# A gated Mamba block with routed experts on one core: every batch in halves of 256 steps, narrower TensorE sums and paired GpSimd products

## The reference

```
xi = in_proj_w @ ctx                      # 512 channels
u  = silu(conv4(xi) + conv_b)
x_dbl = x_proj_w @ u                      # dt_lo (16), B (16), C (16)
delta = softplus(dt_proj_w @ dt_lo + b)
state[e,n] = state[e,n]*exp(delta[e]*A[e,n]) + delta[e]*u[e]*B[n]   # each step
y[e] = sum_n state[e,n]*C[n] + D[e]*u[e]
x  = x + tanh(g_xattn) * y * silu(layernorm(x))
```

```
xc = layernorm(x); combine = top2(softmax(xc @ gate_w.T)), shares scaled to sum 1
h  = gelu(wd @ xc + bd) * combine
x  = x + tanh(g_ffn) * (wu @ h + bu + shared expert)
```

## Time and profile before

| | us |
|---|---|
| median of three runs | 680.33 |
| the profiled execution | 678.83 |
| its span (first to last instruction) | 677.1 |
| TensorE matmuls busy (x1772) | 508.2 (75%) |
| VectorE busy (x556) | 509.2 (75%) |
| ScalarE busy (x594) | 347.6 (51%) |
| GpSimd busy (x278) | 496.7 (73%) |
| granted TensorE clock, mean | 0.856 |

### The profile page before, as it was taken

How to read it: one execution, slowest core, us unless ns; L and a number is a source line. 1 busy time by engine, 2 the same in 40 slices (tenths; PEclk the granted TensorE clock), 3 DMA queues, 4 the chain that set the end, 5 groups by cost and what they waited for, 6 DMA issues and landing times.

```text
span 677.1 us, 6131 instructions
## 1 busy us (share of the span) xinstructions
PE 508.2 (75%) x1772; PEld 223.8 (33%) x1772; DVE 509.2 (75%) x556; ACT 347.6 (51%) x594; POOL 496.7 (73%) x278
## 2 busy tenths in 40 slices
PE   5377242323366998797979979787998999998998
PEld 2022010101022333232423423243343344676676
DVE  3553889787889977899999989997688899614311
ACT  2277533343425698634676575533968734265300
POOL 3026999999998969999999999985588969300000
PEclk9586566767588997897999998979898889999799
DMA  8676513031373304234664120263341321200011
GB/s 258 256 255 252 188 58 125 33 122 62 125 248 125 111 25 148 93 117 154 235 213 154 48 78 32 93 233 140 111 135 53 109 74 52 77 1 1 0 55 54
DMA packets 35325, 79.61 MB, mean 118 GB/s; under 512 B 5497, under 2 KB 9145, under 8 KB 35292
## 3 DMA queue, kind: packets, MB, share of 16 engines
q1 hardware_dynamic: 35292, 79.22, 33.8%
HBM read 62.17 MB, written 17.04 MB: 117 GB/s over the span
## 4 chain that ended last, share of the span: by engine, by line
POOL 29%; PE 25%; DVE 19%; issue 18%; ACT 7%; DMA 2%; POOLq 0%; SPq 0%; ACTq 0%; DVEq 0%
POOL ring L834 16%; POOL ring L843 10%; PE wk L1348 10%; DVE decay L1040 5%; PE wk L1334 5%; DVE ring L1040 5%; PE y_ps L1273 4%; PE wk L1289 2%; ACT decay L899 1%; PE wk L1310 1%; DMA b_in<-bc_scratch 1%; POOL dd_out L816 1%; DVE h L1221 1%; DVE ring L1060 1%; ACT h L986 1%
## 5 line engine op out<-in xcount | busy, mean ns | idle before, releaser
L834 POOL TENSOR_TENSOR ring<-dd,b_in 128x1024 f32<-128x1024 f32 x128 | 299.1, 2354 | 13.9 <-DMA dd<-dd_scratch 10.4
L899 ACT ACTIVATE decay<-dd,a_neg 128x511 f32<-128x511 f32 (+2 forms) x320 | 176.5, 590 | 64.2 <-DVE ring L1040 35.1
L843 POOL TENSOR_TENSOR ring<-ring,c_in 128x1024 f32<-128x1024 f32 x64 | 150.4, 2351 | 25.9 <-DVE carry L1052 16.1
L1273 PE MATMUL y_ps<-ring,fold 128*32 128x512 f32 (+1 forms) x640 | 86.0, 677 | 99.4 <-POOL ring L843 97.2
L1040 DVE TENSOR_TENSOR_SCAN ring<-decay,ring 128x1024 f32<-128x1024 f32 x56 | 127.0, 2280 | 20.1 <-ACT decay L899 13.6
L1040 DVE TENSOR_TENSOR_SCAN decay<-decay,ring 128x1024 f32<-128x1024 f32 x56 | 128.0, 2286 | 15.1 <-ACT decay L899 15.1
L1334 PE MATMUL wk<-xc,w_down 128*128 128x512 f32 (+1 forms) x360 | 134.1, 526 | 4.5 <-issue 4.4
L1348 PE MATMUL wk<-h,w_up 128*128 128x512 f32 (+1 forms) x360 | 132.3, 523 | 0.0
L1334 PEld LDWEIGHTS wk<-xc,w_down 128*128 128x128 f32 x360 | 68.0, 194 | 66.8 <-issue 60.8
L1348 PEld LDWEIGHTS wk<-h,w_up 128*128 128x128 f32 x360 | 68.8, 196 | 54.2 <-issue 49.3
L1060 DVE TENSOR_TENSOR ring<-decay,c_in 128x1024 f32<-128x1024 f32 x64 | 78.4, 1225 | 6.7
(11 more groups left out here) (97 smaller groups left out, 441.1 us busy)
## 6 DMA issues: line engine op xcount, KB each, us to landing
dd<-dd_scratch SPq DMA_DIRECT2D x48, 512.0 KB, 3.8
dd<-dd_scratch SPq DMA_DIRECT2D x32, 256.0 KB, 2.9
dd_scratch<-dd_out SPq DMA_DIRECT2D x12, 512.0 KB, 2.9
z<-in_x SPq DMA_DIRECT2D x4, 1024.0 KB, 6.2
x<-in_xT SPq DMA_DIRECT2D x4, 1024.0 KB, 5.8
c_in<-bc_scratch SPq DMA_DIRECT2D x8, 512.0 KB, 4.9
b_in<-bc_scratch SPq DMA_DIRECT2D x8, 512.0 KB, 5.0
x_scratch<-x SPq DMA_DIRECT2D x3, 1024.0 KB, 8.7
```

Source lines behind the costliest of these rows:

```text
L834: nc.gpsimd.tensor_tensor(ring[:, i % RING].rearrange("p (q n) -> p q n", n=n), dd[:, j % DD_RING, None, n:2 * n].broadcast_to([P, TILES[v ...
L843: nc.gpsimd.tensor_tensor(ring[:, i % RING], ring[:, i % RING], c_in[:, g % BC_RING], ALU.mult).then_inc(weighed_pool, 1)
L899: last = nc.scalar.activation(decay[:, i % 2, q * n + first:(q + 1) * n], dd[:, j % DD_RING, first:n], ACT.Exp, scale=a_neg[:, c, r, k:k + 1])
L1273: last = nc.tensor.matmul(y_ps[r * BLOCK:(r + 1) * BLOCK, 0:n], fold[:], ring[:, slots[r] % RING, q * n:(q + 1) * n], start=False, stop=p ...
```

## The change

Three things at once. Every batch is cut into two units of 256 columns, so there are eight units of 16 slots, and all due times are new; `ring` gets 10 slots, `dd_out` 3, `b_in` and `c_in` 2, and GpSimd works four slots ahead. GpSimd handles two slots in one instruction, for the outer products (`outers`) and for the weighing, which is now of `r` = 0 and 1, and copies the carry for its two slots itself. TensorE computes mean, variance and logits as four partial sums in four groups of 32 columns, which ScalarE copies to SBUF and a second matmul adds up, and `D*u` with four 32x32 diagonals. At the start the loads of z and x leave the fixed first group and are placed by the plan behind the first loads of `dd`, as are the biases and the FFN's weights, which stood ahead of all of them. The rest of the diff:

```diff
-UNITS = [(0, 0, 512), (1, 0, 512), (2, 0, 512), (3, 0, 256), (3, 256, 256)]
+UNITS = [(0, 0, 256), (0, 256, 256), (1, 0, 256), (1, 256, 256), (2, 0, 256), (2, 256, 256), (3, 0, 256), (3, 256, 256)]
-RING = 9
+RING = 10
-DD_OUT = 4
-BC_RING = 3
+DD_OUT = 3
+BC_RING = 2
-AHEAD = 3
+AHEAD = 4
-POOL_WEIGHS = (1, 2)
+POOL_WEIGHS = (0, 1)
...
     "load_ffn": [
-        [-12.75, -11.61, -11.52, -11.43, -11.35, -11.26, -11.17, -11.08, -11, -10.91, -10.82],
+        [-1.56, -0.25, 0.07, 0.21, 0.91, 2.61, 3.65, 5.02, 5.39, 5.6, 6.75],
...
     "dt read": [
+        [0.667, 0.75, 0.833, 0.917],
+        [11.4, 11.6, 11.8, 12.5],
+        [21.5, 21.667, 21.833, 23.333],
...
     "silu": [
+        [0.5],
+        [9.333],
+        [20.5],
...
-            def outer(i):
+            def outers(i):
                 v, c, p, r = PLACES[i]
                 j, g, n = block_no(v, c, r), bc_no(v, p), COLS[v]
-                pool.wait_ge(dd_loaded[j % DD_RING], DMA * (j // DD_RING + 1))
+                for k in (j, j + 1):
+                    pool.wait_ge(dd_loaded[k % DD_RING], DMA * (k // DD_RING + 1))
                 pool.wait_ge(b_loaded[g % BC_RING], DMA * (g // BC_RING + 1))
                 if i >= RING:
-                    pool.wait_ge(summed, (i - RING) // NR4 + 1)
...
+                    pool.wait_ge(summed, (i + 1 - RING) // NR4 + 1)
+                nc.gpsimd.tensor_tensor(ring[:, i % RING:i % RING + 2].rearrange("p s (q n) -> p s q n", n=n),
+                                        dd[:, j % DD_RING:j % DD_RING + 2, None, n:2 * n].broadcast_to([P, 2, TILES[v], n]),
...
             def weigh(i):
...
+                if goes_on(v):
+                    j, k = c * NR4 + r, p * TILES[v]
+                    nc.gpsimd.tensor_copy(carry[:, j - 1:j + 1, k:k + TILES[v], None],
+                                          two.rearrange("p s (q n) -> p s q n", n=n)[:, :, :, n - 1:n]).then_inc(carried, 1)
+                    copies[0] += 1
+                    pool.wait_ge(carried, copies[0])
+                nc.gpsimd.tensor_tensor(two, two, c_in[:, None, g % BC_RING].broadcast_to([P, 2, WIDE]),
+                                        ALU.mult).then_inc(weighed_pool, 2)
...
+            def evacuate_sums(name, v):
...
+                nc.scalar.activation(part_sum[:, 0:COLS[v]], wk[:, bank, 0:COLS[v]], ACT.Copy).then_inc(drained[bank], 1)
...
                 else:
+                    if weighs_on_pool(i):
+                        dve.wait_ge(carried, carries(i))
                     for q in range(TILES[v]):
...
-                if goes_on(v):
+                if goes_on(v) and not weighs_on_pool(i):
...
-                    nc.tensor.matmul(y_ps[:, 0:n], d_diag[:, c, :], u[:, w % U_RING, 0:n], start=True, stop=False)
+                    for r in range(NR4):
+                        rows = slice(r * BLOCK, (r + 1) * BLOCK)
+                        nc.tensor.matmul(y_ps[rows, 0:n], d_diag[rows, c, :], u[rows, w % U_RING, 0:n], start=True, stop=False)
...
-                if name == "mean":
+                if name == "mean_p":
                     for j in range(NW):
                         pe.wait_ge(x2_ready, NW * v + j + 1)
-                        last = nc.tensor.matmul(o, mean_w, x2[:, j, cols], start=j == 0, stop=j == NW - 1)
+                        last = nc.tensor.matmul(o[j * BLOCK:(j + 1) * BLOCK, :], mean_w, x2[:, j, cols], start=True, stop=True)
...
+                if name in ("mean", "var"):
+                    wait_drained(pe, name + "_p", v)
+                    last = nc.tensor.matmul(o, group_w, part_sum[:, 0:n], start=True, stop=True)
```

More of the change, by code:

```diff
@@ L103, in weighs, with carries @@
     return sum(weighs_on_pool(j) == pool for j in range(i))
+def carries(i):
+    v, c, p, r = PLACES[i]
+    k = ((p + 1) * TILES[v] - 1) // TILES[v - 1]
+    return sum(goes_on(PLACES[j][0]) and j % NR4 == POOL_WEIGHS[1] for j in range(slot_of(v - 1, c, k, NR4 - 1) + 1))
 def block_no(v, c, r):
@@ L152 @@
+        [84.96, 85.14, 85.66, 86.91],
+        [105.02, 105.16, 106.02, 107.17],
+    ],
+    "mean_p": [
+        [19.22],
+        [33.81],
+        [52.06],
+        [66.64],
+        [82.31],
+        [100.75],
+        [112.9],
+        [131.26],
     ],
     "mean": [
[L154 to L158, removed]
+        [20.59],
+        [34.58],
+        [54.07],
+        [67.36],
+        [83.44],
+        [101.61],
+        [114.4],
+        [132.62],
+    ],
@@ L159 @@
+    "var_p": [
+        [21.36],
+        [35.47],
+        [55.22],
+        [68.93],
+        [84.77],
+        [103.54],
+        [115.48],
+        [133.39],
     ],
     "var": [
[L161 to L165, removed]
+        [22.72],
+        [36.9],
+        [56.67],
+        [70.11],
+        [86.1],
+        [104.83],
+        [118.43],
+        [133.69],
     ],
     "lg_t": [
-        [44.93],
-        [75.18],
-        [104.2],
@@ L342 @@
+        [107.4, 107.6, 107.8, 109.25],
+    ],
+    "mean_p read": [
+        [21.333],
+        [36.5],
+        [54.667],
+        [69.25],
+        [84.667],
+        [103.333],
+        [115.5],
+        [128.053],
     ],
     "square": [
-        [38.5],
-        [74.333],
-        [103.5],
-        [128.03],
-        [128.121],
+        [22.667],
+        [37.2],
+        [57.25],
+        [69.75],
+        [86.333],
+        [104.667],
+        [117.333],
+        [128.105],
+    ],
+    "var_p read": [
+        [23.667],
+        [37.6],
+        [57.75],
+        [71.5],
+        [87.143],
+        [105.667],
+        [117.667],
+        [128.158],
@@ L476, in by_slot @@
     return due
-JOBS = ("in_proj", "x_proj", "dt", "mean", "var", "lg_t", "lg", "comb", "down", "mix", "up")
+JOBS = ("in_proj", "x_proj", "dt", "mean_p", "mean", "var_p", "var", "lg_t", "lg", "comb", "down", "mix", "up")
 PE_ORDER = in_order("y", *JOBS)
 SP_ORDER = in_order("ctx", "z", "x", "xdbl", "dd", "load_dd", "load_b", "load_c", "load_ffn", "x2_store", "x_out", "out")
-POOL_DUE = by_slot("affine_z", "du", "residual")
-ACT_DUE = by_slot("in_proj read", "silu", "x_proj read", "dt read", "square", "var read", "lg_t read", "share_exp",
+POOL_DUE = by_slot("affine_z", "du", "residual", "weigh")
+ACT_DUE = by_slot("in_proj read", "silu", "x_proj read", "dt read", "mean_p read", "square", "var_p read", "var read", "lg_t read", "share_exp",
                   "comb read", "down read", "gelu")
@@ L530, in mamba_moe_kernel @@
         rank = sb("rank", [P, NX])
-        consts = sb("consts", [P, 7])
-        gates = consts[:, 5:7]
-        eps, minus_half, minus_one, one_of_dm, one = (consts[:, k:k + 1] for k in range(5))
-        mean_w = one_of_dm.broadcast_to([P, P])
+        consts = sb("consts", [P, 8])
+        gates = consts[:, 6:8]
+        eps, minus_half, minus_one, one_of_dm, one, one_of_block = (consts[:, k:k + 1] for k in range(6))
+        mean_w = one_of_dm.broadcast_to([P, BLOCK])
+        group_w = one_of_block.broadcast_to([P, P])
         zeros = sb("zeros", [P, STATES, 1])
@@ L1315, in job @@
                     for j in range(NW):
[L1316 removed]
+                        last = nc.tensor.matmul(o[j * BLOCK:(j + 1) * BLOCK, :], gate_w[:, j, :], xc[:, j, cols], start=True, stop=True)
                 if name == "lg":
@@ L1319, in job @@
                     for t in range(n // P):
-                        last = nc.tensor.transpose(o[:, t * NX:(t + 1) * NX],
-                                                   lg_t[:, cols.start + t * P:cols.start + (t + 1) * P], ident[0:NX, 0:NX])
+                        last = nc.tensor.matmul(o[:, t * NX:(t + 1) * NX],
+                                                lg_t[:, cols.start + t * P:cols.start + (t + 1) * P], lg_sum[:], start=True, stop=True)
                 if name == "comb":
```

559 lines of the change are left out of this document (353 added, 206 removed), and 72 rows, old and new, of the table PLAN.

## The result

The changed kernel takes 701.36 us (median of 4 runs, 696.99 to 706.46) where the kernel before takes 679.09 beside it: **1.033 times as long** (95% interval 1.026 to 1.041). The forecast was 691, with a range of 665 to 716. The profiled execution lasted 701.45 us, with a span of 699.7. (Two executions far outside the rest are left out of the ratios: one of the kernel before beside e1, 700.64 us, and the profiled one of e7, 2669.93 us, whose trace is not read.)

A forecast was written before the change was run, and what follows sets the result against it. VectorE and GpSimd were taken to share the bound, with TensorE bounding the tail. Start 36.5, slots 588 and tail 64 gave 688.5 us, plus 1.7 (span to time) and 1.5 (median of runs): 691, range 665 to 716.

The forecast's parts named there:

- Start, 36.5: Time before the first scan: first scan at 36.5 us, 20.2 us less, bounds 33 and 41.
- Slots, 588: First scan to last weighing: 546 us of VectorE work plus 42 of waits, 588 for 526.6.
- the bias split, 4 by its seven small steps (estimate): VectorE in the slots: the bias split's seven small steps add 4 us, an estimate.
- VectorE's total: Sign over the whole kernel: VectorE busy near 585 us in all, its waits named mostly ScalarE `decay`.
- GpSimd, 478: GpSimd's busy time falls from about 490 to 478 us.
- 60 beside 68 us a unit: GpSimd's load in the slots: its pressure falls, to 60 us beside 68 us a unit.
- ScalarE, 481: ScalarE goes from 348 to about 481 us: exponentials 60 more, table loads 46, smaller pieces about 28.
- Tail, 64: From the last weighing to the end: 64 us for 93.8, bounds 58 and 69.
- Pairing, "17 us less" on GpSimd: GpSimd's outer products and weighings: half as many instructions of 2048 elements save 96 x 0.18 = 17 us.
- Faster: Rival for the slots: less GpSimd load leaves 24 us of waits, 673 us in all; chance 0.32.
- ScalarE sets the pace: Rival for the slots: the whole stream loses 14%, as unit 3 did, 737 us in all; chance 0.15.
- GpSimd still bound: Rival for the slots: GpSimd's 478 us stay below VectorE's 546, so costs only in the first unit; no separate chance.

The follow-up runs named there:

- e1: Changed kernel with the bias split's seven VectorE steps and its loads moved ahead of the first scan; 683.93 us, 1.005 of the kernel before.
- e7: Changed kernel with early bias split, mean and variance again as eight accumulated passes without partial sums; 687.68 us, 1.013 of the kernel before.
- e0: The changed kernel repeated as it is; 700.38 us, 1.029 of the kernel before.
- e2: Changed kernel with early bias split, every paired GpSimd product issued as two of 1024; 684.49 us, 1.008 of the kernel before.
- e6: Units and thick sums of the kernel before, with the change's paired products, GpSimd carry copies and 32-wide diagonals; 672.13 us, 0.989 of the kernel before.
- e9: Changed kernel with early bias split, one more unread 256-column exponential on ScalarE per slot; 696.43 us, 1.024 of the kernel before.
- e8: Changed kernel with early bias split, one more pair of blocks per unit weighed on GpSimd; 707.57 us, 1.041 of the kernel before.
- e11: Changed kernel with early bias split, all FFN weight loads issued right behind the bias rows; 685.08 us, 1.011 of the kernel before.

## Why the prediction was right, and where it was not

The direction and the range held: slower, 701.4 against 691, inside 677 to 705. By its own steps:

- **Start, 36.5: it was 38.4** (36.0 in the repeat, e0). The timeline after:

```profile
16.55 3.48 PE L1539 MATMUL wk<-u,xp_w 128*48 128x256 f32 x8 [3.39 <-ACT u L1145]
...
30.00 2.46 SPq L858 DMA_DIRECT2D dd<-dd_scratch  x4
...
38.38 2.29 DVE L1278 TENSOR_TENSOR_SCAN ring<-decay,ring 128x1024 f32<-128x1024 f32 x1 [22.15 <-POOL ring L1050]
```

  x_proj ended at 20.0 (forecast 21), the first `dd` load was issued at 30.0 (28.5), and the first pair of products started at 33.86 (32).
- **Slots, 588: 593.4.** The 546 us of VectorE's work and the 42 of waits were 541.2 and 52.2. That they add up so well is luck: three errors nearly cancel. **The term that failed is "the bias split, 4 by its seven small steps (estimate)": it took 18.3.** The price was read where GpSimd was idle, and the step moved to where it is not. Without it the slots take 575.2 us (e1), 523.4 of work and 51.9 of waits, where the rest of the sum had 542 and 42: the work was 19 too high, the waits 10 too low. The work was added up from single pieces, and neighbouring instructions overlap in the trace: in e1 the durations of VectorE's instructions in the slots add up to 562.9 us and cover 523.4. How much of the 19 is that was not taken apart.
- **VectorE's total.** The sign "near 585 us in all" did not come; it was 561.8. Nor were its waits "mostly" for `decay`: 12.8 us of 52.2 are named so, the largest part but a quarter.
- **GpSimd, 478.** It was 477.9 in the slots, its product 4.532 for 4.53. But it had been 478.55 there before, so its load in the slots did not fall. Its products take 11 us less in the slots (439 before, 428 after), the `du` and residuals 6 more, the carry copies and the small steps of z's normalisation 4 more. The "60 beside 68 us a unit" is a wrong reading: the earlier trace rows give 61.4, 60.4, 66.3 and 54.8 us for 16 slots of units 1 to 4.
- **ScalarE, 481: 446.9.** The table loads came as counted, 80 for 79. The exponentials are busy 212.5 us, not 237: neighbouring ones overlap in the trace, so a mean duration times a count exceeds the busy time (in the earlier trace rows too, 192 x 0.676 = 130 for 123.5). The forecast took busy times for before (177) and mean times count for after, so its "60 more" should have been 36. The drain that the Trainium skill states for a change of table (ScalarE: Activation LUTs, What ACT_TABLE_LOAD costs) does not show here either. ScalarE is idle 0.6 us in all before these 32 loads, and behind a load the next instruction starts after 0.01 us (median of 79):

```profile
L1092 ACT ACT_TABLE_LOAD x32 | 41.1, 1283 | 0.6
```

- **Tail, 64: 67.9.** Three `up` jobs of unit 6 were left instead of two (629.77, 636.50 and 641.36), the first of them half done at 631.83. The logits began 20.8 us behind the last weighing, not 17.5; they and `down` took 1.7 us more than forecast, the last `up` jobs 1 less:

```profile
629.77 4.15 PE L1594 MATMUL wk<-h,w_up 128*128 128x256 f32 x18
...
641.36 4.15 PE L1594 MATMUL wk<-h,w_up 128*128 128x256 f32 x18
```

- **Pairing, "17 us less" on GpSimd:** the size was right (15.4 by e2), its worth in this kernel nothing that the runs can tell. The forecast did not say that a part of the change without the halves could beat both kernels, which e6 does.
- **The rivals.** *Faster* (673) needed waits under 27 us in the slots. They fell from 64.7 to 52.2 only (51.9 without the bias split), and GpSimd's load there, whose fall it built on, stayed as it was. *ScalarE sets the pace* (737) fell: e9 gives ScalarE 48 us more and loses 12.5. *GpSimd still bound* fell by e2, but only in sum: in e8, with 36 us more, GpSimd's place in the order costs 24.

## What to carry over

When a step is moved from an idle stretch into a busy one, its price has to be read again: here seven VectorE instructions of 4.4 us in all cost 18 beside GpSimd, and putting them back gave 16.5 us of the 19.8 that the change lost there. A shorter start or tail is worth only the idle time of the bounding engine in it; what that engine did there comes back in the slots (26.8 of the 44.2 us here). And slack summed over a kernel is not slack at the moment when another engine waits: 36 us more on an engine with 98 to spare in the slots cost 24, in the one order tried.

## What was not expected of the hardware

In these traces a VectorE instruction whose inputs are both in SBUF, or a cast or `tensor_scalar` from SBUF to SBUF, stood still until GpSimd's current instruction had ended: 4.60 to 4.87 us beside products of 4.53, 2.44 to 2.71 beside products of 2.35, against 0.42 to 0.74 by themselves. VectorE's scans (one large input in `decay`, which is PSUM, one in `ring`) show nothing of it: 0.73 us in both kernels. Between two queued GpSimd instructions one VectorE step gets in, and then the next GpSimd instruction: with the short products six of seven steps were caught, the last five in a row. And a store of 32 KB, issued 4 us behind the last of 4.7 MB of loads, took 6.0 us instead of 1.5 (e11 and e1).
